# A graph layer's gathered rows: one quarter group in every third round, instead of every sixth, fetched row by row from two other queues

## The reference

```
h    = relu(layernorm(x))                            # 12500 x 128
cat  = concatenate(h[src], h[dst], edge_attr)        # 200000 x 384
msg  = relu(cat @ W1 + b1)                           # 200000 x 128
aggr = segment_sum(msg, dst, 12500)
out  = x + layernorm(aggr + h) * gamma + beta
```

## Time and profile before

| what | before |
|---|---|
| median of 3 runs | 1951.73 us (1951.48 to 1951.76) |
| profiled execution | span 1949.5 us from first to last instruction; its time outside the span is not given |
| POOL | 75% busy, 1463.9 us |
| PE | 79% busy, granted clock 0.90 on average |
| DVE, ACT | 64%, 34% busy |
| DMA | 306.84 MB, 157 GB/s |
| gathers of line 613 | 1484, 945 ns each |

### The profile page before, as it was taken

The page is one execution under the profiler, slowest core; times in us unless marked ns, Lnnn a source line. Parts: engine busy times, 40 slices in busy tenths (PEclk is TensorE's granted clock), DMA queues, the critical chain, the costliest instruction groups (busy, mean ns, idle before and its releaser), DMA issues.

```text
span 1949.5 us, 52908 instructions
## 1 busy us (share of the span) xinstructions
PE 1548.5 (79%) x11881; PEld 1483.7 (76%) x11881; DVE 1256.9 (64%) x3454; ACT 659.4 (34%) x1507; POOL 1463.9 (75%) x1559
## 2 busy tenths in 40 slices
PE   5688788778878787877787788787788888877887
PEld 5678788777777777877777787777777877777786
DVE  7656666667666666666666676666566665656665
ACT  5533333333333333333333333333323232322323
POOL 7777777777777777777777777777777777777776
PEclk9888888989889998998989998999898888888988
DMA  9755656556565655656565565656556565555554
GB/s 261 204 143 144 167 143 166 152 156 166 144 169 145 164 152 155 163 147 169 149 160 153 155 166 144 168 140 168 147 154 163 138 164 148 155 148 153 163 145 106
DMA packets 229468, 306.84 MB, mean 157 GB/s; under 512 B 46461, under 2 KB 141157, under 8 KB 229317
## 3 DMA queue, kind: packets, MB, share of 16 engines
q1 hardware_dynamic: 151858, 192.55, 34.4%
q0 software_dynamic: 49536, 101.55, 21.4%
q10 hardware_dynamic: 27922, 11.43, 2.7%
HBM read 281.72 MB, written 23.64 MB: 157 GB/s over the span
## 4 chain that ended last, share of the span: by engine, by line
issue 22%; DMA 22%; POOL 20%; PE 13%; DVE 10%; DVEq 8%; ACT 2%; ACTq 2%; POOLq 1%; SPq 0%
DMA a_rows<-table_a,picks 20%; POOL a_rows L613 19%; DVEq L1398 5%; DVE onehot_cols L1367 3%; PE ps_pre L769 3%; PE ps_pre L770 3%; PE ps_sum L781 2%; DVE msg L1387 2%; PE ps_edge L756 2%; PE ps_fin L781 1%; DVE aggr L1408 1%; ACTq L1027 1%; DMA table_a<-a_out 1%; DVEq L1383 1%; PE ps_sum L788 1%
## 5 line engine op out<-in xcount | busy, mean ns | idle before, releaser
L613 POOL DMA_INDIRECT a_rows<-table_a,picks x1484 | 1401.8, 945 | 452.4 <-issue 400.3
L769 PE MATMUL ps_pre<-w_c,edge_cols 128*128 128x128 f32 x3128 | 671.5, 300 | 29.5 <-issue 29.2
L770 PE MATMUL ps_pre<-b_win,onehot_cols 128*128 128x128 f32 x3128 | 663.2, 297 | 0.0
L995 ACT ACTIVATE msg<-msg 128x512 f32<-128x512 f32 x390 | 245.7, 630 | 951.9 <-DVE msg L1387 893.1
L769 PEld LDWEIGHTS ps_pre<-w_c,edge_cols 128*128 128x128 f32 x3128 | 537.1, 215 | 38.6 <-issue 37.0
L1387 DVE TENSOR_TENSOR msg<-ps_pre,a_rows 128x512 f32<-128x512 f32 x374 | 257.0, 687 | 433.8 <-DMA a_rows<-table_a,picks 339.4
L770 PEld LDWEIGHTS ps_pre<-b_win,onehot_cols 128*128 128x128 f32 x3128 | 534.7, 214 | 0.0
L1367 DVE SCALAR_TENSOR_TENSOR onehot_cols<-space,base_all,ps_hot 64x512 f32<-64x512 int32 x391 | 438.3, 1121 | 0.6 <-DMA space<-in_dst 0.6
L781 PE MATMUL ps_sum<-onehot,msg 128*128 128x64 f32 x1560 | 214.6, 283 | 105.2 <-ACT e_rows L1013 71.3
L781 PEld LDWEIGHTS ps_sum<-onehot,msg 128*128 128x128 f32 x1560 | 200.5, 201 | 123.4 <-ACT e_rows L1013 82.2
L991 ACT ACTIVATE edge_cols<-ps_edge 128x512 f32<-128x512 f32 x391 | 228.4, 584 | 136.8 <-PE ps_edge L756 115.7
(11 more groups left out here) (137 smaller groups left out, 1073.8 us busy)
## 6 DMA issues: line engine op xcount, KB each, us to landing
edges<-in_edge_attr SPq DMA_DIRECT2D x195, 512.0 KB
space<-in_dst SPq DMA_DIRECT2D x195, 256.0 KB
a_rows<-table_a,picks POOLq DMA_INDIRECT x1484
hand_rows<-table_a SPq DMA_DIRECT2D x1024, 0.5 KB
hand_rows<-table_a ACTq DMA_DIRECT2D x1024, 0.5 KB
b_win<-table_b SPq DMA_DIRECT2D x391, 32.0 KB
table_b<-b_rows ACTq DMA_DIRECT2D x96, 64.0 KB
out<-out_rows SPq DMA_DIRECT2D x96, 64.0 KB
```

Of the source, the lines that this page charges most:

```text
L613: pool.indirect_dma_start(a_rows[:, u, k, :], None, table_a[:, :], bass.IndirectOffsetOnAxis(ap=picks[:, u, k:k + 1], axis=0),).then_inc(s ...
L769: pe.matmul(to, edge_cols[:, u % 2, k * P:(k + 1) * P], w_c[:, :], start=True, stop=False)
L770: mm = pe.matmul(to, onehot_cols[:, u % 2, k * P:(k + 1) * P], b_win[:, u, :], start=False, stop=True)
L995: act.activation(msg[:, u % 2, :, :], msg[:, u % 2, :, :], ACT.Relu).then_inc(s_msg, 1)
```

## The change

- `PERIOD` becomes 3: each third round has a hand quarter (k = 3 of group u = 0), so there are 32 instead of 16; with one for the last group (its fourth quarter) 33. POOL's gathers of line 613 fall from 1484 to 1467. The early groups stay in each sixth round.
- Of a quarter's 128 rows SP fetches 72 (nine batches of eight, three in each of the three rounds) and ACT 56 (seven batches of eight). All go into one buffer `hand_rows`; the first batch of each waits until the hand quarter before has been added (`hand_used`).
- SP's and ACT's loops run over three rounds. The body of SP's has some 286 instructions (406 before), that of ACT's first loop some 243 (395 before).
- SP issues a pair of windows after one wait instead of two waits, and loads the twelve window starts of three rounds at once from `base_sp`. DVE loads the four offsets of a round at once from `base_dve`, instead of one before each addition of sums.
- Several semaphores are merged: one per u for gathered rows, and `s_turn_rows` and `s_last_rows`.
- The last group: POOL gathers three quarters (`last_step`), DVE adds the hand quarter first, then quarters 0 and 1, then 2; PE and ACT follow in that order. SP and ACT fetch its 128 rows in rounds 96 and 97.

```diff
-PERIOD = 6
+PERIOD = 3
-ACT_ROWS = 64
+ACT_ROWS = 56
...
-                def window(i, u, base):
...
+                def windows(i, h, base, end=PAIR):
...
                     if past(i, 1):
-                        sp.wait_ge(s_pre, (i - 1) * UNROLL + u + 1)
+                        sp.wait_ge(s_pre, (i - 1) * UNROLL + h * PAIR + end)
                     sp.sem_inc(s_gate_sp, 1)
-                    sp.dma_start(b_win[0:WIN, u, :], table_b[bass.ds(base, WIN), :]).then_inc(s_b_win[u], 16)
+                    for u in range(h * PAIR, h * PAIR + end):
+                        sp.dma_start(b_win[0:WIN, u, :], table_b[bass.ds(base[u], WIN), :]).then_inc(s_b_win[u], 16)
...
+                SLOTS = ((None, 0, 1, 2), (3, 4, 5, None), (6, 7, 8, None))
+                assert SP_ROWS == 9 * BATCH
+
+                def rounds(t):
+                    base = load_bases(mybir.EngineType.SP, base_sp, t * PLACE, PERIOD * UNROLL)
+                    for j in range(PERIOD):
+                        round_(t * PERIOD + j, base[j * UNROLL:(j + 1) * UNROLL], t, SLOTS[j])
...
                 with sp.Fori(1, EARLY_GROUPS) as s:
-                    rounds(s)
-                round_(ROUNDS - 2)
-                base = bases(ROUNDS - 1)
+                    with sp.Fori(0, 2) as n:
+                        rounds(s * 2 + n)
+                    load_early(s)
+                base = load_bases(mybir.EngineType.SP, base_sp, HANDS * PLACE, 2 * UNROLL)
+                round_(ROUNDS - 2, base[0:UNROLL], HANDS, SLOTS[0])
                 pair(ROUNDS - 1, 0)
-                for u in range(LEFT):
-                    if u == PAIR:
-                        tail()
-                    window(ROUNDS - 1, u, base[u])
+                fetch(HANDS, 3)
+                windows(ROUNDS - 1, 0, base[UNROLL:])
+                fetch(HANDS, 4)
+                tail()
+                fetch(HANDS, 5)
+                windows(ROUNDS - 1, 1, base[UNROLL:], LEFT - PAIR)
+                for batch in range(6, SP_ROWS // BATCH):
+                    fetch(HANDS, batch)
...
-                for u in range(LEFT):
+                for u in range(LEFT - 1):
                     step(ROUNDS - 1, u)
+                last_step(ROUNDS - 1, LEFT - 1)
...
+                NEXT, SLOTS = ((), (), (0,), ()), (((1,), (), (2,), (3,)), ((4,), (), (5,), (6,)))
...
-                round_(ROUNDS - 1, LEFT)
-                last_relu(1, 0, SUB - 1)
+                round_(ROUNDS - 1, LEFT, t=HANDS, slots=((4,), (5, 6), ()))
+                last_relu(1, HAND_K, SUB)
+                last_relu(2, 0, HAND_K - 1)
...
                 dve.wait_ge(s_pre, GROUPS)
                 dve.wait_ge(s_sum, GROUPS - 2)
-                last_add(0, SUB - 1)
-                add_sums(ROUNDS - 1, LEFT - 2)
-                base = base_of(GROUPS - 1)
+                hands_landed(HANDS + 1)
+                last_add(HAND_K, SUB, hand_rows[:, :])
+                for k in range(HAND_K - 1):
+                    dve.wait_ge(s_last_rows[k], 16)
+                last_add(0, HAND_K - 1, a_rows[:, LEFT - 1, 0:HAND_K - 1, :].rearrange("p k f -> p (k f)"))
+                add_sums(ROUNDS - 1, LEFT - 2, base[LEFT - 1])
```

More of the change, by code:

```diff
@@ L511, in round_ @@
-                def round_(i, t=None, par=None, j=None):
-                    base = bases(i)
-                    for u in range(UNROLL):
-                        if u % PAIR == 0:
-                            pair(i, u // PAIR)
-                        window(i, u, base[u])
-                        if t is not None and (j, u) in SP_SLOTS:
-                            fetch(t, par, SP_SLOTS.index((j, u)))
+                    numbers = hand_numbers(mybir.EngineType.SP, t, batch)
+                    for p in range(BATCH):
+                        sp.dma_start(hand_row(batch * BATCH + p), row_at(numbers[p])
+                                     ).then_inc(s_hand_sp[0 if batch < FIRST_BATCHES else 1], 16)
@@ new lines, in round_ @@
+                def round_(i, base, t=None, slots=(None,) * 4):
+                    pair(i, 0)
+                    if slots[0] is not None:
+                        fetch(t, slots[0])
+                    windows(i, 0, base)
+                    if slots[1] is not None:
+                        fetch(t, slots[1])
+                    pair(i, 1)
+                    if slots[2] is not None:
+                        fetch(t, slots[2])
+                    windows(i, 1, base)
+                    if slots[3] is not None:
+                        fetch(t, slots[3])
@@ L1033, in round_ @@
                             columns(*after(i, u, 1))
-                        if t is not None and j * UNROLL + u < len(ACT_SLOTS) and ACT_SLOTS[j * UNROLL + u]:
-                            fetch(t, par, j * UNROLL + u)
+                        for batch in slots[u]:
+                            fetch(t, batch)
                         if u == 3 and past(i, 2):
@@ new lines, in _ @@
+                for j in range(PERIOD - 1):
+                    plain_round(0, 0, j, True)
+                hand_round(0, 0, True)
+                rounds(0, 1, True)
+                half = EARLY_ROWS // EARLY
+                with dve.Fori(1, half) as s:
+                    with dve.Fori(0, 2) as n:
+                        rounds(s, n, True)
+                rounds(half, 0, True)
+                for j in range(PERIOD - 1):
+                    plain_round(half, 1, j, PERIOD + j < EARLY_REST)
@@ L1506, in last_add @@
+                hand_round(half, 1, False)
+                with dve.Fori(half + 1, EARLY_GROUPS) as s:
+                    with dve.Fori(0, 2) as n:
+                        rounds(s, n, False)
+                plain_round(EARLY_GROUPS, 0, 0, False)
+                base = round_(ROUNDS - 1, (EARLY_GROUPS * (EARLY - 2) + 2, None), LEFT)
+                def last_add(first, end, rows):
                     dve.tensor_tensor(msg[:, (LEFT - 1) % 2, first:end, :].rearrange("p k f -> p (k f)"),
-                                      ps_pre[(LEFT - 1) % 2][:, first * H:end * H],
```

247 lines of the change are left out of this document (136 added, 111 removed).

## The result

| | before | changed kernel |
|---|---|---|
| median | 1951.61 us (1951.41 to 1951.76, 4 runs) | 1964.97 us (1963.83 to 1967.19, 4 runs) |
| ratio | 1 | 1.0071 (1.0057 to 1.0085) |
| profiled execution | span 1949.5 | span 1962.0, its time 1963.83 |

A forecast was written before the change was run, and what follows sets the result against it. POOL, gathering without a gap, was taken to bound the kernel. Gathers -21.2 and tail +4.3 gave -16.9 us, so span 1932.6 and, with 2.2 between span and median, 1934.8 us; range 1930 to 1944.

The forecast's parts named there:

- Gathers: On POOL, 17 fewer gathers at 1.2495 us each: 21.2 us less, if POOL still never waits.
- SP's work: On SP's queue, 108 us of work in six rounds of 112.5 us, leaving 4 to 5 us spare.
- DVE's base loads: On DVE, one load of four offsets replaces four of one, off the path: nothing, except at the end.
- one wait for two windows: On SP, a pair's first window comes when the second used to; products need it several us later: nothing.
- The hand rows in time: Hand rows land one or two us before DVE needs them, with POOL's 3.7 behind: nothing counted.
- Loops of three rounds: SP's jumps back, twice as many over shorter bodies: 0 to 5 us of SP's time in six rounds, taken as 0.
- The tail: At the end, SP's last hand rows delay DVE's last additions: +4.3 us, range +2.9 to +6.7.
- ACT, "nothing counted": ACT's batches ahead of `e_cols` or a relu delay it by 3.4 us, covered by POOL's 3.7: nothing counted.
- POOL's 3.7: Spare us between DVE's addition of a group and POOL's gathers overwriting its rows, read after the short round.
- Rival C: POOL stalls a little after short rounds, 0.15 to 1 us, 16 times; 1937 to 1951 us, chance 0.17.
- Rival D: SP becomes the bound, needing 115.7 us for six rounds against POOL's 112.5; 1967 to 1986 us, chance 0.10.

The follow-up runs named there:

- experiment 1: Changed kernel with ACT's batch of the fourth group (u = 3) issued behind the copy to `e_cols` instead of ahead of it: 1935.03 us, ratio 0.9921.
- experiment 9: Changed kernel, ACT's batch behind `e_cols`, last group's fourth quarter gathered by POOL; windows wait singly, DVE loads offsets singly: 1935.97 us, ratio 0.9902.
- experiment 8: Kernel of experiment 1 with SP's loop body holding six rounds (some 580 instructions) instead of three inside a loop of two: 1947.56 us, ratio 0.9970.
- the 16 matmuls: Changed kernel with 16 more PE matmuls ahead of its wait for `e_cols`, in two of three early rounds: 1935.88 us, ratio 0.9917.
- 12 matmuls: Changed kernel with 12 more PE matmuls ahead of its wait for `e_cols` in rounds 0 to 63: 1964.11 us, ratio 1.0039.
- experiment 6: Changed kernel with extra PE matmuls ahead of its wait for `e_cols`: 24 gave 2014.77 us, 12 gave 1964.11, 16 in two of three rounds 1935.88.

## Why the prediction was wrong

- **Gathers, -21.2:** right. With POOL not waiting (experiment 1) the last gather starts 20.6 us earlier than before.
- **SP's work, 108 us for six rounds:** right on the whole. Its waits fell to 93 us, and it bore the load in experiment 1, but with 3.6 us to spare in six rounds and not the 4 to 5 I gave it: a load of eight addresses took 0.92 in the median, not 0.76, so that a batch was at 3.6, the upper end.

```profile
L369 SPq TENSOR_LOAD <-hand_picks x297: 527/915/1154, 77.0 to 1948.9; - x149
```

- **DVE's base loads and one wait for two windows, nothing each:** right (experiment 9). No run undoes the merged semaphores by themselves.
- **The hand rows in time, nothing:** right for the time, since POOL has no stall in experiment 1. But one or two us to spare was too much: there DVE waited for them 16 times, 25.4 us in all and up to 3.9.
- **Loops of three rounds, 0:** near enough. The two jumps cost SP 0.6 to 0.8 us in six rounds, and undoing the short body costs more than I said (experiment 8). The old jump was dearer than the 2.5 us that I read: the trace of before shows 4.4 to 5.1 us there 14 times, and 1.30 where SP enters the loop without a jump, at 191.20. The rule of the Trainium skill, in "Runtime: NRT & Kernel Launch", section "Instruction fetch mechanics", spoke against bodies of 286 instructions only if they lie badly; here their jumps cost some tenths of a us, and one over a body twice as long costs 3.3.
- **The tail, +4.3:** right in mechanism and size, +4.2. The last row was issued at 1952.3 and DVE added at 1953.48, so that it landed within 1.2 us, not 1.6.
- **ACT, "nothing counted":** this is the step that failed. I wrote that two batches in three rounds stand ahead of `e_cols` or a relu "and delay it by 3.4; the addition a round later moves by about as much, and POOL's 3.7 cover it". Two things were wrong in it. First, a delay that comes back in two of every three rounds isn't to be held against a cover that was read once: it lengthens the chain's period, here to 116.1 us, and the period is what has to be compared with POOL's 112.5 us for six rounds. Cover only puts off when POOL first stalls by more than tenths, here to 427 us. Secondly, the 4 us or so that PE waits are not the whole price; the halved clock behind them adds some 3 us of PE's time. With as late a start of the sums but without the slow clock (the 16 matmuls) three rounds took 53.7 us instead of 58.0, and POOL's pace all but held. The prediction had no term for the clock. Rival C named the place and the "short rounds", and priced it at 0.15 to 1 us each time, where 3.6 came; it took three mishaps to meet there, where one was enough. Rival D, SP as the bound, named the wrong engine.

The chances were 0.10 for slower. The profile of before had what was needed: ACT's stream shows four rows ahead of `e_cols`, and PE stands behind that copy. It even shows what the clock does behind a short wait for another copy of ACT:

```profile
687.84 1.12 PE L781 MATMUL ps_sum<-onehot,msg 128*128 128x64 f32 x8 [1.48 <-ACT e_rows L1013]
688.78 1.04 PE L756 MATMUL ps_edge<-ident,edges 128*128 128x128 f32 x4
689.61 0.63 PE L769 MATMUL ps_pre<-w_c,edge_cols 128*128 128x128 f32 x2
```

The transposes take 1.04 and the products 0.63, where 0.60 and 0.39 are the full clock's.

## What to carry to other kernels

When work is added to an engine's queue, look at what stands behind it and who waits for that, and compare periods, not one delay with one slack: a cover is spent once, a delay in a loop comes back. Put issue work behind the instruction that another engine waits for; here that move of three lines turned +0.7% into -0.8%. A wait of TensorE of a few us is dearer than it looks wherever the granted clock drops behind it, so read the clock by windows around the wait before pricing it.

## What the runs showed of the hardware

- TensorE's granted clock stood at 0.50 behind a wait of 3.1 us in which it did nothing (the changed kernel, 920.7 to 926.7; so too behind 27 more waits of 3.7 to 4.1), and also behind one of 1.5 us that followed 2.8 us of matmuls, but not behind one of 1.1 us that did so (12 matmuls); with the wait filled by 3.7 us of matmuls up to its last 0.2 it stayed at 1.00.
- 24 float32 matmuls of 128x64 took 5.47 us and appear as 48 instructions, 12 took 2.79 (experiment 6).
- A jump back over a body of some 580 instructions on SP's queue cost about 3.3 us (experiment 8), over some 406 about 3.4 (the kernel before: 4.68 in the median, less 1.30), over some 286 instructions 0.3 to 0.5 (experiment 1).
- A load of eight addresses into SP's registers took 0.92 us in the median in the changed kernel, where SP issues 9 batches in three rounds, and 0.76 before, where it issues 4; what makes the difference is not shown.
